# A graph network's four hops: the products and totals on VectorE take their factor from an SBUF column instead of the instruction

## The chip, the core and the metric

The kernel runs on one core of a Trainium2 chip. The metric is the time of one execution on the device in microseconds (us), the median over the runs. The times of single instructions come from one further execution, which the hardware profiler recorded.

## The reference, cut to what matters

Two graph layers follow each other on 50000 nodes with 128 features and 25000 edges (`src`, `dst`). The first layer gives each edge a message, adds the messages up by node, and multiplies with a weight matrix; a layer norm follows. The second layer is the one whose code is changed:

```python
src2 = concat([src, dst]); dst2 = concat([dst, src]); e2 = concat([e, e])      # 50000 directed edges, 4 heads
e2 = e2 / segment_sum(e2, dst2)[dst2]
def f(y): return segment_sum(y[src3] * e3, dst3)      # edges from a node to itself count zero
k1 = f(x); k2 = f(x + k1/3); k3 = f(x + k2 - k1/3); k4 = f(x + k1 - k2 + k3)
y = x + 0.125 * (k1 + 3*(k2 + k3) + k4)
```

Because `f` is linear, the result is a sum of powers of `f`: x + f(x) + f(f(x))/2 + f³(x)/6 + f⁴(x)/24. The kernel computes four such applications in turn and calls each a hop. A last layer norm gives the output.

## The kernel before, in words

A first part (until about 1840 us) sorts the directed edges by the node that they end in, computes the first layer, and builds the tables for the hops. The sorted edges lie as 128 rows of C = 392 columns. Then come four hops (`hop(h)`, h = 0 to 3), and after about 4100 us the last layer norm, in which GpSimd gathers rows once more (L1128).

A hop goes over NB = 49 batches of B = 8 columns, so 128 x 8 edges of 128 features. Each engine has its own list of instructions, written out by hand, and they are tied by semaphores.

- GpSimd (POOL in the profile) issues one indirect DMA per column (L1004), which gathers the 128 rows of the edges' other ends from HBM into one of four buffers `gx`. It may run up to four batches ahead of VectorE (it waits for `z_set`).
- VectorE (DVE) waits for the eight gathers of a batch, then multiplies them by the edge weights `wt` into `zt`. In hop 0 this is four instructions of 128x256 (L1041, one per head, with no wait between them), in hops 1 to 3 one of 128x1024 (L1046). These are called the first product here.
- Then VectorE adds along the row of edges that end in the same node: eight instructions of 128x128 (L1056), the running sums. Each waits for the one before. Their factor is a column of the tile `cont` in SBUF.
- Then one 128x1024 product with `inv` into `us` (L1061), and in hops 1 to 3 the total, `tn = us * share + tp`, again 128x1024 (L1068).
- SyncE (SP) writes `us` and `tn` to HBM and loads `tp`.

All of these are the VectorE instruction `scalar_tensor_tensor`: out = (in0 op factor) op in1. It reads two tensors, both from SBUF here, and a factor. The factor is either a number in the instruction or one value per partition, read from a [128, 1] column in SBUF.

Of the kernel before, what the change touches and what calls it, by code (L numbers as in the profile page):

```python
# [65 lines left out]
def build(nc, x, src, dst, e_in, ea_in, Wf, bf, Wq, Wk, Wa, Wu, bu, out):  # L66
# [9 lines left out]
    with ExitStack() as ctx:  # L76
        def sb(name, shape, dt=F32, stage=None):
            return (stage or ctx).enter_context(nc.sbuf_tensor(name, shape, dt))
# [9 lines left out]
        part = sb("part", [128, Q])  # L88
        after = sb("after", [128, 128])
        ones = sb("ones", [128, ST])  # L90
        first_row = sb("first_row", [128, 128])
        eps_t = sb("eps_t", [128, 1])
        key = sb("key", [128, 2 * NT])
# [15 lines left out]
        wt = sb("wt", [128, C, H])  # L109
        inv = sb("inv", [128, C, H])  # L110
# [64 lines left out]
        with nc.Block() as block:  # L175
# [108 lines left out]
            def _(v):  # L284
# [2 lines left out]
                v.memset(srt[0][:, :], PAD).then_inc(code_set, 1)  # L287
                v.memset(ones[:, :], 1.0).then_inc(const_set, 1)
                v.memset(eps_t[:, :], EPS)
                v.wait_ge(iota_done, 3)  # L290
                v.tensor_copy(pos[:, :], pos_i[:, :]).then_inc(code_set, 1)
                v.tensor_copy(part[:, :], part_i[:, :]).then_inc(code_set, 1)
# [70 lines left out]
                for k in range(1, 17):  # L363
                    v.wait_ge(srt_set, n)
                    t = srt[a]
# [37 lines left out]
                for n in range(NHG):  # L403
                    if n >= 2:
                        v.wait_ge(counted, n - 1)
                    for i in range(HG):
# [3 lines left out]
                        t = v.tensor_scalar(hot_lo[n % 2][:, i, :], pos_h[0:EP, :], part_f[:, 1, c:c + 1], None,  # L410
                                            ALU.is_equal)
# [510 lines left out]
        us = [sb(f"us{i}", [128, B, D], F32, held) for i in range(3)]  # L922
        tp = [sb(f"tp{i}", [128, B, D], F32, held) for i in range(3)]
        tn = [sb(f"tn{i}", [128, B, D], F32, held) for i in range(3)]
# [10 lines left out]
        def hop(h):  # L935
# [4 lines left out]
            share = (1.0, 0.5, 1.0 / 6, 1.0 / 24)[h]  # L940
# [7 lines left out]
            def slot(b, m, n):  # L948

                return n * ((NB - 1 - b % m) // m + 1) + b // m  # L950
# [7 lines left out]
            def by_head(t):  # L958
                return t[:, :, :].rearrange("p j (h f) -> p (j h) f", h=H)

            def per_head(w, cs):
                return w[:, cs, :].rearrange("p j h -> p (j h)").unsqueeze(2).to_broadcast([128, B * H, HF])

            def gxv(i):
                return gx[i][:, 0:B * width].rearrange("p (j f) -> p j f", j=B)

            with nc.Block() as block:
                @block.sync
                def _(sp):
                    for b in range(NB + 1):  # L970
                        if h and b < NB:
                            if b >= 3:
                                sp.wait_ge(tn_set, t0 + b - 2)
                            sp.dma_start(tp[b % 3][:, :, :], rows(so_far, b)).then_inc(t_in[b % 3], 16)
                        if b >= 1:
                            k = b - 1
                            if h < 3:
                                sp.wait_ge(us_set, done + k + 1)
                                sp.dma_start(rows(u[h], k), us[k % 3][:, :, :]).then_inc(u_out[k % 3], 16)
                            if h:  # L980
                                sp.wait_ge(tn_set, t0 + k + 1)
                                sp.dma_start(rows(target, k), tn[k % 3][:, :, :]).then_inc(t_out[k % 3], 16)
                    sp.wait_ge(x_set, x0 + 3)
                    if h < 3:
                        sp.dma_start(u[h][XROW:XROW + 128, :], cross[:, :]).then_inc(x_out, 16)
                        for i in range(3):
                            sp.wait_ge(u_out[i], outs(i, h))
                    else:
                        sp.dma_start(target[XROW:XROW + 128, :], cross[:, :]).then_inc(x_out, 16)
                    if h:  # L990
                        for i in range(3):
                            sp.wait_ge(t_out[i], outs(i, h - 1))
                    sp.wait_ge(x_out, h * 16 + 16)
# [38 lines left out]
                @block.vector  # L1032
                def _(v):
                    for b in range(NB):
                        cs = slice(b * B, (b + 1) * B)
                        z = zt[b % 2]
                        v.wait_ge(g_in[b % 4], (slot(b, 4, h) + 1) * B * 16)
                        if h == 0:
                            for i in range(H):
                                f = slice(i * HF, (i + 1) * HF)  # L1040
                                t = v.scalar_tensor_tensor(z[:, :, f], gxv(b % 4)[:, :, f], 1.0,  # L1041
                                                           wt[:, cs, i].unsqueeze(2).to_broadcast([128, B, HF]),
                                                           ALU.mult, ALU.mult)
                            t.then_inc(z_set, 1)
                        else:
                            v.scalar_tensor_tensor(by_head(z), by_head(gxv(b % 4)), 1.0, per_head(wt, cs),  # L1046
                                                   ALU.mult, ALU.mult).then_inc(z_set, 1)
                        v.wait_ge(z_set, done + b + 1)
                        for j in range(B):
                            c = b * B + j  # L1050
                            if c == 0:
                                continue
                            prev = z[:, j - 1, :] if j else zt[1 - b % 2][:, B - 1, :]
                            if c >= 2:
                                v.wait_ge(run_set, run0 + c - 1)
                            v.scalar_tensor_tensor(z[:, j, :], prev, cont[:, c:c + 1], z[:, j, :], ALU.mult, ALU.add  # L1056
                                                   ).then_inc(run_set, 1)
                        v.wait_ge(run_set, run0 + b * B + B - 1)
                        if h < 3 and b >= 3:
                            v.wait_ge(u_out[b % 3], slot(b, 3, h) * 16)  # L1060
                        v.scalar_tensor_tensor(by_head(us[b % 3]), by_head(z), 1.0, per_head(inv, cs),  # L1061
                                               ALU.mult, ALU.mult).then_inc(us_set, 1)
                        if h:
                            v.wait_ge(t_in[b % 3], slot(b, 3, h - 1) * 16 + 16)
                            if b >= 3:
                                v.wait_ge(t_out[b % 3], slot(b, 3, h - 1) * 16)
                            v.wait_ge(us_set, done + b + 1)
                            v.scalar_tensor_tensor(tn[b % 3][:, :, :], us[b % 3][:, :, :], share, tp[b % 3][:, :, :],  # L1068
                                                   ALU.mult, ALU.add).then_inc(tn_set, 1)

                    v.wait_ge(carried, h + 1)
                    v.tensor_tensor(cross[:, :].rearrange("p (h f) -> p h f", h=H),
                                    bank[0][:, 0:D].rearrange("p (h f) -> p h f", h=H),
                                    inv_first[:, :].unsqueeze(2).to_broadcast([128, H, HF]), ALU.mult
                                    ).then_inc(x_set, 1)
                    v.wait_ge(x_set, x0 + 1)
                    v.scalar_tensor_tensor(cross_sum[:, :], cross[:, :], share, cross_sum[:, :], ALU.mult, ALU.add
                                           ).then_inc(run_set, 1)
                    v.wait_ge(first_in, h * 16 + 16)
                    v.wait_ge(run_set, run0 + C)  # L1080
                    if h < 3:
                        v.tensor_tensor(cross[:, :], cross[:, :], first_u[:, :], ALU.add).then_inc(x_set, 2)
                    else:
                        v.tensor_tensor(cross[:, :], cross_sum[:, :], first_u[:, :], ALU.add).then_inc(x_set, 2)
# [90 lines left out]
```

## Time and profile before

| | |
|---|---|
| median of 3 runs | 4589.34 us (4587.24 to 4590.71) |
| profiled execution, its own time | 4611.0 us |
| its span (first to last instruction) | 4608.9 us |
| VectorE busy | 2438.1 us (53%) |
| GpSimd busy | 3161.3 us (69%) |
| first gather of hop 0, last gather of hop 3 | 1840.2 us, 4080.7 us |

Busy time is the time in which an engine executes an instruction; the short pauses in which GpSimd prepares the next DMA do not count as busy. An engine's idle time matters only where another engine waits for it.

### The profile page before, as it was taken

The page shows a single profiled execution, that of the slowest core. Times are in us where ns is not written, and L with a number is a line of the kernel's source. Part 1 is how long each engine was busy: PE and PEld are TensorE (multiplying, and loading weights), DVE is VectorE, ACT ScalarE, POOL GpSimd, SP SyncE. Part 2 cuts the span into 40 slices and gives each one's busy share as a digit, 9 for nine tenths or more (in the row PEclk, how much of TensorE's full clock was granted, in tenths as well). Part 3 has the DMA queues.
Part 4 walks back from the last instruction along what each step waited for, and adds up shares of the span by engine and source line. Part 5 has one row for each costly group of instructions (what it writes and reads, how often), then busy time and mean ns, then how long its engine had stood idle before and what let it go on. Part 6 is the DMA issues. An engine that isn't in the chain of part 4 may idle for free. (4 is left out here: it accounts for less than half of the span.)

```text
span 4608.9 us, 25791 instructions
## 1 busy us (share of the span) xinstructions
PE 930.8 (20%) x5636; PEld 763.5 (17%) x5636; DVE 2438.1 (53%) x7329; ACT 608.4 (13%) x1752; POOL 3161.3 (69%) x2952
## 2 busy tenths in 40 slices
PE   0364666665667700000000000000000000000000
PEld 0123556555545500000000000000000000000000
DVE  6895444444468902455445555455554555543333
ACT  0001111111147810000000000000000000003333
POOL 0004877877867775777767777677776777767776
PEclk9997877788789955555555555555555555555555
DMA  8002333333357810333335555455554444445555
GB/s 249 13 1 54 64 65 69 65 66 69 60 168 246 256 26 4 95 99 96 99 100 187 188 183 183 157 188 183 183 189 147 138 139 144 140 122 157 157 160 142
DMA packets 294505, 581.90 MB, mean 126 GB/s; under 512 B 118824, under 2 KB 147294, under 8 KB 294349
## 3 DMA queue, kind: packets, MB, share of 16 engines
q1 hardware_dynamic: 172669, 383.36, 24.5%
q0 software_dynamic: 116128, 169.55, 18.4%
q10 hardware_dynamic: 5552, 27.34, 1.8%
q8 instruction: 44, 0.72, 0.1%
q14 instruction: 112, 0.92, 0.1%
HBM read 332.26 MB, written 247.75 MB: 126 GB/s over the span
## 5 line engine op out<-in xcount | busy, mean ns | idle before, releaser
L1004 POOL DMA_INDIRECT gx<-u,far_row x1176 | 1290.0, 1097 | 391.6 <-issue 357.8
L1056 DVE SCALAR_TENSOR_TENSOR zt<-zt,cont 128x128 f32<-128x128 f32 x1564 | 551.2, 352 | 55.5
L1046 DVE SCALAR_TENSOR_TENSOR zt<-gx,wt 128x1024 f32<-128x1024 f32 x147 | 180.5, 1228 | 682.2 <-DMA gx<-u,far_row 682.2
L1004 POOL DMA_INDIRECT gx<-x,far_i x392 | 405.6, 1035 | 147.6 <-issue 119.2
L552 POOL DMA_INDIRECT xs<-in_x_dram,node_idx x196 | 195.9, 999 | 438.2 <-POOLq L175 378.8
L800 POOL DMA_INDIRECT edge_s<-edge_d,edge_id x392 | 376.0, 959 | 141.0 <-issue 132.1
L1021 PE MATMUL bank<-zt,chain 128*128 128x128 f32 x8 | 3.2, 501 | 2267.1 <-DVE zt L1056 2267.1
L1128 POOL DMA_INDIRECT o_ag<-total,fin_idx x390 | 369.9, 948 | 129.9 <-issue 118.6
L1021 PEld LDWEIGHTS bank<-zt,chain 128*128 128x128 f32 x8 | 2.0, 312 | 2268.1 <-DVE zt L1056 2268.1
L544 POOL DMA_INDIRECT agg<-summed,sc_idx x196 | 316.6, 1615 | 81.1 <-issue 58.1
L734 ACT ACTIVATE o_log_v<-o_mv,eps_t 128x6 f32<-128x6 f32 x66 | 19.7, 299 | 2052.8 <-DVE o_mv L727 2052.8
L647 DVE TENSOR_SCALAR neg<-bank 128x512 f32<-128x512 f32 x49 | 33.9, 692 | 485.1 <-PE bank L597 485.1
L1061 DVE SCALAR_TENSOR_TENSOR us<-zt,inv 128x1024 f32<-128x1024 f32 x196 | 240.0, 1224 | 6.8
L556 POOL DMA_INDIRECT xd<-in_x_dram,node_idx x196 | 201.0, 1026 | 59.8 <-issue 59.8
L1148 DVE SCALAR_TENSOR_TENSOR o_res<-o_xc,o_ag 128x768 f32<-128x768 f32 x66 | 62.6, 948 | 317.6 <-issue 285.0
L1041 DVE SCALAR_TENSOR_TENSOR zt<-gx,wt 128x256 f32<-128x256 f32 x196 | 70.3, 420 | 250.0 <-DMA gx<-x,far_i 250.0
L1068 DVE SCALAR_TENSOR_TENSOR tn<-us,tp 128x1024 f32<-128x1024 f32 x147 | 180.2, 1226 | 20.8 <-DVE us L1061 0.5
L574 PE MATMUL bank<-za,same 128*128 128x132 f32 x1568 | 184.6, 276 | 3.0 <-DVE za L680 3.0
L574 PEld LDWEIGHTS bank<-za,same 128*128 128x128 f32 x1568 | 180.2, 190 | 3.2 <-issue 3.2
L753 ACT ACTIVATE normed<-res,shift,rstd 128x128 f32<-128x128 f32 x391 | 156.8, 480 | 0.0
L753 ACT ACTIVATE o_normed<-o_res,o_shift,o_rstd 128x128 f32<-128x128 f32 x391 | 156.4, 478 | 0.0
L410 DVE TENSOR_SCALAR hot_lo<-pos_h,part_f 125x512 f16<-125x512 f16 x400 | 139.3, 348 | 0.0
(182 smaller groups left out, 3140.9 us busy)
## 6 DMA issues: line engine op xcount, KB each, us to landing
u<-us SPq DMA_DIRECT2D x147, 512.0 KB, 2.6
total<-tn SPq DMA_DIRECT2D x147, 512.0 KB, 3.3
tp<-total SPq DMA_DIRECT2D x98, 512.0 KB, 5.2
agg<-zero ACTq DMA_DIRECT2D x49, 544.5 KB
ag<-agg SPq DMA_DIRECT2D x65, 396.0 KB
x<-normed SPq DMA_DIRECT2D x65, 387.0 KB
o_xc<-x SPq DMA_DIRECT2D x65, 387.0 KB, 5.0
tp<-u SPq DMA_DIRECT2D x49, 512.0 KB, 5.9
```

The lines of the kernel that those rows point to most:

```text
L544: g.indirect_dma_start(agg[:, :], bass.IndirectOffsetOnAxis(ap=sc_idx[:, s * Q + j:s * Q + j + 1], axis=0), summed[s % 2][:, j, :], None, ...
L552: g.indirect_dma_start(xs[s % 3][:, j, :], None, x[:, :], bass.IndirectOffsetOnAxis(ap=node_idx[:, s * Q + j:s * Q + j + 1], axis=0)).then ...
L556: g.indirect_dma_start(xd[s % 3][:, j, :], None, x[:, :], bass.IndirectOffsetOnAxis(ap=node_idx[:, c:c + 1], axis=0)).then_inc(x_in[s % 3] ...
L574: t = pe.matmul(r_bank[b // 2][:, b % 2 * AW:(b % 2 + 1) * AW], same[s % 2][:, a, b * 128:(b + 1) * 128], za[s % 2][:, a, :], start=(a == ...
L753: t = act.activation(normed[s % 2][0:P, r, 0:D], res[s % 4][0:P, r, :], ACT.Identity, bias=shift[s % 4][0:P, r:r + 1], scale=rstd[s % 4][0 ...
L800: g.indirect_dma_start(edge_s[:, c, :], None, edge_d[:, :], bass.IndirectOffsetOnAxis(ap=edge_id[:, c:c + 1], axis=0)).then_inc(edge_in, 16)
L1004: g.indirect_dma_start(gx[b % 4][:, j * width:(j + 1) * width], None, source[:, :], bass.IndirectOffsetOnAxis(ap=idx[:, c:c + 1], axis=0)) ...
L1046: v.scalar_tensor_tensor(by_head(z), by_head(gxv(b % 4)), 1.0, per_head(wt, cs), ALU.mult, ALU.mult).then_inc(z_set, 1)
L1056: v.scalar_tensor_tensor(z[:, j, :], prev, cont[:, c:c + 1], z[:, j, :], ALU.mult, ALU.add).then_inc(run_set, 1)
L1061: v.scalar_tensor_tensor(by_head(us[b % 3]), by_head(z), 1.0, per_head(inv, cs), ALU.mult, ALU.mult).then_inc(us_set, 1)
L1068: v.scalar_tensor_tensor(tn[b % 3][:, :, :], us[b % 3][:, :, :], share, tp[b % 3][:, :, :], ALU.mult, ALU.add).then_inc(tn_set, 1)
L1128: g.indirect_dma_start(ag[s % 4][0:P, r, 0:D], None, total[2][:, :], bass.IndirectOffsetOnAxis(ap=at, axis=0)).then_inc(o_row[s % 4], 16)
```

## The change

The number 1.0 in the three products (L1041, L1046, L1061) becomes the first column of `ones`, a tile that the kernel already has. The number `share` in the total (L1068) becomes a column of a new 128x4 tile `shares`, which four small memsets fill at the program's start. What is computed stays the same. No instruction is moved on any engine, none is taken away, and the four memsets are the only ones added. The new tile moves the tiles allocated behind it by 32 bytes.

```diff
+        shares = sb("shares", [128, 4])
...
                 v.memset(eps_t[:, :], EPS)
+                for i in range(4):
+                    v.memset(shares[:, i:i + 1], (1.0, 0.5, 1.0 / 6, 1.0 / 24)[i])
                 v.wait_ge(iota_done, 3)
...
-                                t = v.scalar_tensor_tensor(z[:, :, f], gxv(b % 4)[:, :, f], 1.0,
+                                t = v.scalar_tensor_tensor(z[:, :, f], gxv(b % 4)[:, :, f], ones[:, 0:1],
                                                            wt[:, cs, i].unsqueeze(2).to_broadcast([128, B, HF]),
                                                            ALU.mult, ALU.mult)
...
-                            v.scalar_tensor_tensor(by_head(z), by_head(gxv(b % 4)), 1.0, per_head(wt, cs),
+                            v.scalar_tensor_tensor(by_head(z), by_head(gxv(b % 4)), ones[:, 0:1], per_head(wt, cs),
                                                    ALU.mult, ALU.mult).then_inc(z_set, 1)
...
-                        v.scalar_tensor_tensor(by_head(us[b % 3]), by_head(z), 1.0, per_head(inv, cs),
+                        v.scalar_tensor_tensor(by_head(us[b % 3]), by_head(z), ones[:, 0:1], per_head(inv, cs),
                                                ALU.mult, ALU.mult).then_inc(us_set, 1)
...
-                            v.scalar_tensor_tensor(tn[b % 3][:, :, :], us[b % 3][:, :, :], share, tp[b % 3][:, :, :],
+                            v.scalar_tensor_tensor(tn[b % 3][:, :, :], us[b % 3][:, :, :], shares[:, h:h + 1], tp[b % 3][:, :, :],
                                                    ALU.mult, ALU.add).then_inc(tn_set, 1)
```

## Rows read from the trace of the kernel before

**Rows 1.** Page, part 1: busy us, share of the span, instructions.

```profile
PE 930.8 (20%) x5636; PEld 763.5 (17%) x5636; DVE 2438.1 (53%) x7329; ACT 608.4 (13%) x1752; POOL 3161.3 (69%) x2952
```

**Rows 2.** Waits, 1840 to 4100 us: us in total, times, longest.

```profile
DVE zt L1046 <- DMA gx<-u,far_row: 682.2, 147, 20.6
POOL gx L1004 <- issue: 477.0, 1564, 0.3
```

**Rows 3.** Groups, 1840 to 4100 us: busy us, mean ns | idle before.

```profile
L1004 POOL DMA_INDIRECT gx<-u,far_row x1176 | 1290.0, 1097 | 391.6 <-issue 357.8 <-ACTq L967 33.8
L1056 DVE SCALAR_TENSOR_TENSOR zt<-zt,cont 128x128 f32<-128x128 f32 x1564 | 551.2, 352 | 55.5
L1004 POOL DMA_INDIRECT gx<-x,far_i x392 | 405.6, 1035 | 147.6 <-issue 119.2 <-POOLq L781 28.4
...
L1046 DVE SCALAR_TENSOR_TENSOR zt<-gx,wt 128x1024 f32<-128x1024 f32 x147 | 180.5, 1228 | 682.2 <-DMA gx<-u,far_row 682.2
...
L1041 DVE SCALAR_TENSOR_TENSOR zt<-gx,wt 128x256 f32<-128x256 f32 x196 | 70.3, 420 | 250.0 <-DMA gx<-x,far_i 250.0
...
L1077 DVE SCALAR_TENSOR_TENSOR cross_sum<-cross,cross_sum 128x128 f32<-128x128 f32 x4 | 1.2, 292 | 0.1
```

**Rows 4.** Timeline, one batch of hop 3: start us, us, engine, line.

```profile
3738.52 1.23 DVE L1046 SCALAR_TENSOR_TENSOR zt<-gx,wt 128x1024 f32<-128x1024 f32 x1 [4.35 <-DMA gx<-u,far_row]
3739.05 1.52 POOL L1004 DMA_INDIRECT gx<-u,far_row  x1 [0.30 <-issue]
...
3742.89 1.22 DVE L1061 SCALAR_TENSOR_TENSOR us<-zt,inv 128x1024 f32<-128x1024 f32 x1
3743.38 1.55 POOL L1004 DMA_INDIRECT gx<-u,far_row  x1 [0.30 <-issue]
3744.25 1.23 DVE L1068 SCALAR_TENSOR_TENSOR tn<-us,tp 128x1024 f32<-128x1024 f32 x1
3745.23 1.06 POOL L1004 DMA_INDIRECT gx<-u,far_row  x1 [0.30 <-issue]
...
3749.77 1.23 DVE L1046 SCALAR_TENSOR_TENSOR zt<-gx,wt 128x1024 f32<-128x1024 f32 x1 [4.29 <-DMA gx<-u,far_row]
```

**Rows 5.** Timeline, one batch of hop 0.

```profile
1958.68 1.43 DVE L1041 SCALAR_TENSOR_TENSOR zt<-gx,wt 128x256 f32<-128x256 f32 x4 [5.01 <-DMA gx<-x,far_i]
1959.80 1.13 POOL L1004 DMA_INDIRECT gx<-x,far_i  x1 [0.30 <-issue]
...
1963.25 1.22 DVE L1061 SCALAR_TENSOR_TENSOR us<-zt,inv 128x1024 f32<-128x1024 f32 x1
1963.74 1.55 POOL L1004 DMA_INDIRECT gx<-x,far_i  x1 [0.30 <-issue]
```

**Rows 6.** Timeline before the hops; L859's factor is a column.

```profile
1317.36 0.61 DVE L859 SCALAR_TENSOR_TENSOR xa<-ag,decay,xc 128x128 f32<-128x128 f32 x2
...
1317.73 1.06 POOL L800 DMA_INDIRECT edge_s<-edge_d,edge_id  x1 [0.30 <-issue]
```

**Rows 7.** Timeline, a gather that starts just behind an L1056.

```profile
3340.42 0.41 DVE L1056 SCALAR_TENSOR_TENSOR zt<-zt,cont 128x128 f32<-128x128 f32 x1
3340.51 0.95 POOL L1004 DMA_INDIRECT gx<-u,far_row  x1 [0.31 <-issue]
...
3551.11 0.35 DVE L1056 SCALAR_TENSOR_TENSOR zt<-zt,cont 128x128 f32<-128x128 f32 x1
3551.23 1.05 POOL L1004 DMA_INDIRECT gx<-u,far_row  x1 [0.30 <-issue]
```

**Rows 8.** Timeline, a gather that starts just behind an L1046.

```profile
2648.25 1.22 DVE L1046 SCALAR_TENSOR_TENSOR zt<-gx,wt 128x1024 f32<-128x1024 f32 x1 [6.08 <-DMA gx<-u,far_row]
2648.30 2.00 POOL L1004 DMA_INDIRECT gx<-u,far_row  x1 [0.30 <-issue]
```

**Rows 9.** Timeline, at the program's start.

```profile
5.09 0.06 DVE L289 MEMSET eps_t<- 128x1 f32 x1
```

**Rows 10.** Waits, 9 to 24 us: us in total, times, longest.

```profile
DVE rows_f L322 <- DMA rows_i<-in_dst_dram: 13.6, 1, 13.6
```

## The prediction, made before the changed kernel was run

> **What bounds the kernel now.** I read the page first: GpSimd is busy 69% of the span, more than any other engine [rows 1]. Then the waits of the four hops, 1840 to 4100 us. Before a gather GpSimd waits only for its own issue, 0.30 us each, 477 us over 1564 gathers; apart from the hops' first gathers it waits for no other engine. VectorE in turn waits 682 us for gathers in front of L1046 [rows 2]. So the hops last as long as GpSimd needs for 1568 gathers.
>
> Then the groups: a gather takes 1097 ns on average in hops 1 to 3 and 1035 ns in hop 0 [rows 3], but the undisturbed ones in the timeline take 0.95 us [rows 7]. The timeline shows where the rest comes from. In a batch of hop 3 a gather starts at 3739.05, inside L1046, which ends at 3739.75. It takes 1.52 us and ends at 3740.57, 0.82 behind L1046's end. The one at 3743.38 starts inside L1061 (end 3744.11) and ends at 3744.93, again 0.82 behind. The one at 3745.23 starts inside L1068 (end 3745.48) and ends at 3746.29, 0.81 behind [rows 4]. So a gather that starts while such a VectorE instruction runs stands still until it ends, and then needs its last 0.82 us. A free gather would have reached this point 0.95 - 0.82 = 0.13 us after its start.
>
> Over the batch that is 0.57 + 0.60 + 0.11 = 1.28 us lost, and 8 x (0.95 + 0.30) + 1.28 = 11.28 us, against 3749.77 - 3738.52 = 11.25 measured [rows 4]. Over all, the stops cost 1176 x (1.097 - 0.947) + 392 x (1.035 - 0.947) = 176 + 34 = 211 us, with 0.947 for the 0.95. The running sums have the very form of the changed ones, and 60 is my value.
>
> **Does the column form stop GpSimd too?** Yes: L859 takes its factor from a column. Two of them end at 1317.97; the gather of 1317.73 takes 1.06 us and ends at 1318.79, 0.82 behind [rows 6]. So do the running sums: a gather that starts 0.12 us behind the start of an L1056 (3551.11, end 3551.46) takes 1.05 us and ends 0.82 behind that end [rows 7].
>
> The Trainium skill, SBUF — State Buffer, section "Who interferes with whom", says that an instruction with two SBUF inputs contends with GpSimd's reads only, and infers that issuing a DMA, which needs the write side, isn't stopped by it. By that rule the stops and with them the change would cost nothing; the rows say otherwise, and they decide.
>
> **Hops 1 to 3.** Take the batch of rows 4 with 60 ns more on each of L1046, L1061 and L1068. The gather in L1046 is released 0.06 later. The next gathers and the running sums both hang on that end, so their distance stays, and a gather again starts 0.49 into L1061, whose end is now 0.12 later. Again both sides hang on that end, and L1068 releases GpSimd 0.18 later. Where no gather falls into L1046 the sum is the same, since L1061 and L1068 still stop one and their ends are 0.12 and 0.18 later against the batch's start. 147 batches x 0.18 = 26.5 us.
>
> One thing works against it: which engine is first. In the immediate form a gather that starts 0.05 behind L1046's start is already stopped (2.00 us) [rows 8]; in the column form one at 0.09 goes free and VectorE waits instead (0.41 in place of 0.35), while one at 0.12 is stopped [rows 7]. So the tensors are read about 0.06 later, behind the column. Gathers start every 1.25 us and their place against L1046 varies from batch to batch; if evenly, 0.06 / 1.25 = 5% of 147 batches, 7, now slip in front of L1046 and escape. Each wins about a whole gather, 1.1 us: -8 us. Hops 1 to 3: +18 us.
>
> **Hop 0.** The four L1041 last 1.43 us together: 0.42 the last, and a distance of about 0.34 from start to start (3 x 0.34 + 0.42 = 1.44). A gather starts 1.12 into them, inside the fourth, is released at 1.43 and ends 2.25 behind the batch's start. L1061 starts 3.14 behind the end of the fourth; the gather that it stops starts 3.63 behind that end, so 0.49 into it [rows 5]. With 0.06 more each, the third ends at 2 x 0.40 + 0.48 = 1.28 and the fourth at 1.68. The gather at 1.12 is now in the third, is released at 1.28, and its successor reaches L1061 at 1.28 + 3.63 = 4.91. L1061 begins at 1.68 + 3.14 = 4.82. That is 0.09 inside: exactly where the gather wins the race by rows 7. So two outcomes per batch:
> - Stopped: L1061 ends 4 x 0.06 + 0.06 = 0.30 later and holds GpSimd until then. Batch +0.30; over 49 batches +14.7 us.
> - Escaped: the gather is issued first, the next comes 1.25 later, at 6.16, when L1061 has less than 0.13 left. The batch has no stop but at most 0.1 in the third: 8 x 1.25 + 0.05 = 10.05 us. Before it was 10.0 + 0.18 + 0.60 = 10.78 in rows 5, and by the group's mean 8 x (1.035 + 0.304) = 10.71. So -0.66, over 49 batches -32 us.
>
> Which one depends on where the gather starts. If it comes later than 1.28 - 0.13 = 1.15 it isn't stopped by the third and reaches L1061 at 4.91 to 5.0, up to 0.18 inside, which is stopped. The mean place follows from the group: 34 us over 49 batches is 0.70 a batch, less 0.60 for L1061 is 0.10 at the fourth, so a mean start of 1.43 - 0.13 - 0.10 = 1.20. So somewhat more than half come too late to escape. With a third escaping: 0.67 x 0.30 - 0.33 x 0.66 = -0.02 a batch. Hop 0: 0 us, and I keep +15 and -32 as ends.
>
> **The rest.** The four memsets take 0.06 us each [rows 9] and lie before a wait of VectorE of 13.6 us for `rows_i` [rows 10]: nothing; without this cover 0.24 us. The hops' ends, where VectorE's last batch lies on the path, get 3 x 0.18 + 0.30 = 0.8 us. Tiles that lie 32 bytes further on could change how fast DMAs land; GpSimd waits for no landing within a hop, so it would act only through the places of the gathers against L1046: a few us either way, in the range. Nothing is queued newly behind a wait, and SP's writes leave 0.1 to 0.3 us later, with 11 us between batches.
>
> **Sum.** 18 + 0 + 1 = +19 us: 4611.0 + 19 = 4630 for a profiled execution. That one lies 21.7 above the median of the runs, so 4589.3 + 19 = 4608 us. A measurement of this kernel can tell about 0.2%, 9.2 us, from no change: the bounds are 4580 and 4598.5.
>
> **Rivals.**
> - Hop 0 stays stopped throughout (column cost under 55 ns, or gathers later than I think): 18 + 15 + 1 = +34, up to +42 with no escapes in hops 1 to 3: 4623 to 4631. A cost that grows with the elements lies here too, and above: 480 ns on the 3 x 147 long forms of hops 1 to 3 would be 212 us; I hold it for near nothing. For: a race decided by 10 ns. 0.22.
> - Hop 0 escapes throughout, the one that ends on the other side: at 0.06 or more per L1041, once the gather starts before 1.15 in all batches, GpSimd passes in front of L1061. -32 + 18 + 1 = -13: 4576 us. It is faster from about two thirds of the batches on if the others gain little; against it speaks the mean start of 1.20. 0.09.
> - The gains cancel: part of hop 0 escapes, about half, and more than 7 batches of the other hops: +0 to +9, 4589 to 4598. Also here: the column costs nothing in the long forms. 0.17.
> - The column form doesn't stop GpSimd, as the skill's page would have it for all of them: the 211 us come back but for the running sums, about 4380 us. Rows 6 and 7 speak against it. 0.02.
> - The forecast, 4599 to 4622: 0.50.
>
> **Numbers.** Slower: 0.50 + 0.22 = 0.72. Faster: 0.09 + 0.02 = 0.11. Within 0.2%: 0.17. The range, 4582 to 4631, holds the forecast, the stopped hop 0 and the cancelling, leaves out the full escape, and is that wide because hop 0 has ends of +15 and -32; the forecast's own is 4599 to 4622.
>
> **What would show it.** L1046, L1061 and L1068 at about 1286 ns, L1041 at 480. The gathers' mean in hops 1 to 3: 18 us over 1176 is +15 ns, 1112; up to 1120 without escapes. In hop 0 1035 if a third escapes, 1072 if none, 950 if all; a spread between batches of 10.05 and 11.0 us. Released gathers still end 0.82 behind VectorE's end. After 4100 us nothing changes. Wrong would be: long forms that take 1226 as before, gathers of 0.95 us inside a running L1061, or a hop 0 with one kind of batch only.

## The result and the profile after

The changed kernel takes 4626.35 us (median of 4 runs, 4618.09 to 4634.81), the kernel before 4590.02 us in the same runs (4587.24 to 4596.11). The ratio is 1.0077 with a 95% interval of 1.006 to 1.0094: 28 to 43 us slower, 35 in the middle. The profiled execution took 4634.81 us, its span is 4632.8 us.

The page's groups after the change, each with its busy time in us, the mean of one instruction in ns, and the idle time before them (`...` stands for groups left out):

```profile
L1007 POOL DMA_INDIRECT gx<-u,far_row x1176 | 1298.2, 1104 | 391.3 <-issue 357.6
L1059 DVE SCALAR_TENSOR_TENSOR zt<-zt,cont 128x128 f32<-128x128 f32 x1564 | 551.7, 353 | 55.5
L1049 DVE SCALAR_TENSOR_TENSOR zt<-gx,ones,wt 128x1024 f32<-128x1024 f32 x147 | 189.0, 1285 | 666.7 <-DMA gx<-u,far_row 666.7
L1007 POOL DMA_INDIRECT gx<-x,far_i x392 | 415.1, 1059 | 147.5 <-issue 119.2
...
L1064 DVE SCALAR_TENSOR_TENSOR us<-zt,ones,inv 128x1024 f32<-128x1024 f32 x196 | 252.0, 1286 | 7.0
...
L1044 DVE SCALAR_TENSOR_TENSOR zt<-gx,ones,wt 128x256 f32<-128x256 f32 x196 | 82.2, 480 | 243.6 <-DMA gx<-x,far_i 243.6
L1071 DVE SCALAR_TENSOR_TENSOR tn<-us,shares,tp 128x1024 f32<-128x1024 f32 x147 | 188.7, 1284 | 19.8 <-DVE us L1064 0.5
```

All line numbers are 3 higher than before in the hops. The column costs 60 ns at 256 elements a partition (420 to 480) and 57 at 1024 (1228 to 1285) [rows 3], so it is paid once per instruction and doesn't grow with the length. The running sums, which had a column already, stay at 353. VectorE is busy 39.6 us longer in all (2477.7 us against 2438.1) and still waits 667 us for gathers. The gathers, which set the time, went from 1035 to 1059 ns in hop 0 and from 1097 to 1104 in hops 1 to 3.

A batch of hop 3 in the timeline (start, length):

```profile
3740.87 1.28 DVE L1064 SCALAR_TENSOR_TENSOR us<-zt,ones,inv 128x1024 f32<-128x1024 f32 x1
3741.35 1.62 POOL L1007 DMA_INDIRECT gx<-u,far_row  x1 [0.30 <-issue]
3742.29 1.28 DVE L1071 SCALAR_TENSOR_TENSOR tn<-us,shares,tp 128x1024 f32<-128x1024 f32 x1
3743.28 1.11 POOL L1007 DMA_INDIRECT gx<-u,far_row  x1 [0.30 <-issue]
```

Against [rows 4] the gather starts at the same place in the product, 0.48 us in, takes 1.62 in place of 1.55, and ends at 3742.97, again 0.82 behind the product's end. The one in the total takes 1.11 in place of 1.06.

And hop 0, first a batch of the common kind, then one of the few others:

```profile
2055.16 1.69 DVE L1044 SCALAR_TENSOR_TENSOR zt<-gx,ones,wt 128x256 f32<-128x256 f32 x4 [4.88 <-DMA gx<-x,far_i]
2056.39 0.94 POOL L1007 DMA_INDIRECT gx<-x,far_i  x1 [0.30 <-issue]
...
2060.02 1.28 DVE L1064 SCALAR_TENSOR_TENSOR us<-zt,ones,inv 128x1024 f32<-128x1024 f32 x1
2060.13 1.99 POOL L1007 DMA_INDIRECT gx<-x,far_i  x1 [0.30 <-issue]
...
2066.28 0.48 DVE L1044 SCALAR_TENSOR_TENSOR zt<-gx,ones,wt 128x256 f32<-128x256 f32 x1 [4.97 <-DMA gx<-x,far_i]
```

```profile
1979.35 1.67 DVE L1044 SCALAR_TENSOR_TENSOR zt<-gx,ones,wt 128x256 f32<-128x256 f32 x4 [5.05 <-DMA gx<-x,far_i]
1980.42 1.02 POOL L1007 DMA_INDIRECT gx<-x,far_i  x1 [0.31 <-issue]
...
1984.16 1.34 DVE L1064 SCALAR_TENSOR_TENSOR us<-zt,ones,inv 128x1024 f32<-128x1024 f32 x1
1984.24 0.95 POOL L1007 DMA_INDIRECT gx<-x,far_i  x1 [0.30 <-issue]
...
1989.28 0.88 DVE L1044 SCALAR_TENSOR_TENSOR zt<-gx,ones,wt 128x256 f32<-128x256 f32 x2 [3.78 <-DMA gx<-x,far_i]
```

In the first, the gather of 2056.39 (1.23 us into the four products) isn't stopped at all, and the one that reaches L1064 0.11 behind its start stands for 1.05 us, nearly the whole product: the batch takes 11.12 us, from the start of its first product to that of the next batch. In the second the gather is stopped a little by the third product, reaches L1064 0.08 behind its start, is first, and VectorE waits: 1.34 in place of 1.28; the batch takes 9.93 us. Only 3 of the 49 batches are of this kind, where I had expected a third. In 29 the gather comes 0.10 to 0.13 behind the start of L1064 and stands. In 16 a gather that starts 1.25 to 1.31 into the four products is stopped by the fourth of them, and the gather that reaches L1064 then comes about 0.48 behind its start (once 0.87) and is stopped too. The stopped batches take 10.99 us on average, where the mean before was 10.73.

### The profile page after: what moved, and what is told of

Its sections match the earlier page's. It is cut to its first block and busy times, and to the rows that moved or that the text cites. A ratio compares the mean times of both kernels' runs of the same rounds, so it can differ in the third digit from the quotient of the medians.

```text
span 4632.8 us, 25795 instructions
## 1 busy us (share of the span) xinstructions
PE 943.7 (20%) x5636; PEld 773.4 (17%) x5636; DVE 2477.7 (53%) x7333; ACT 609.0 (13%) x1752; POOL 3175.6 (69%) x2952
## 5 line engine op out<-in xcount | busy, mean ns | idle before, releaser
L1007 POOL DMA_INDIRECT gx<-u,far_row x1176 | 1298.2, 1104 | 391.3 <-issue 357.6
L1049 DVE SCALAR_TENSOR_TENSOR zt<-gx,ones,wt 128x1024 f32<-128x1024 f32 x147 | 189.0, 1285 | 666.7 <-DMA gx<-u,far_row 666.7
L1007 POOL DMA_INDIRECT gx<-x,far_i x392 | 415.1, 1059 | 147.5 <-issue 119.2
L1064 DVE SCALAR_TENSOR_TENSOR us<-zt,ones,inv 128x1024 f32<-128x1024 f32 x196 | 252.0, 1286 | 7.0
L1044 DVE SCALAR_TENSOR_TENSOR zt<-gx,ones,wt 128x256 f32<-128x256 f32 x196 | 82.2, 480 | 243.6 <-DMA gx<-x,far_i 243.6
L1071 DVE SCALAR_TENSOR_TENSOR tn<-us,shares,tp 128x1024 f32<-128x1024 f32 x147 | 188.7, 1284 | 19.8 <-DVE us L1064 0.5
```

Of the source, the lines that this page charges most:

```text
L1007: g.indirect_dma_start(gx[b % 4][:, j * width:(j + 1) * width], None, source[:, :], bass.IndirectOffsetOnAxis(ap=idx[:, c:c + 1], axis=0)) ...
L1049: v.scalar_tensor_tensor(by_head(z), by_head(gxv(b % 4)), ones[:, 0:1], per_head(wt, cs), ALU.mult, ALU.mult).then_inc(z_set, 1)
L1064: v.scalar_tensor_tensor(by_head(us[b % 3]), by_head(z), ones[:, 0:1], per_head(inv, cs), ALU.mult, ALU.mult).then_inc(us_set, 1)
```

## Experiments

In the table and the text below, "gather time" is the gathers' busy time plus their issue pauses in the group's row. For the kernel before it is 405.6 + 119.2 = 524.8 us in hop 0 and 1290.0 + 357.8 = 1647.8 us in hops 1 to 3 [rows 3]; for the changed one 534.3 and 1655.8 us. Each comes from one profile. Profiles of kernels with the same hops 1 to 3 (numbers in the instructions) differ by up to 10 us there (1637.6 to 1647.8), and the first gather starts anywhere from 1831 to 1850 us, whatever the change. So single differences of a few us in one hop say nothing, and the ratio, from several runs each, judges the whole kernel.

| kernel | factor in | hop 0, us | hops 1 to 3, us | ratio to before, 95% |
|---|---|---|---|---|
| before | number | 524.8 | 1647.8 | |
| changed | column | 534.3 | 1655.8 | 1.0077 (1.006 to 1.0094) |
| e1_same_places | column | 537.1 | 1662.5 | 1.0079 (1.0061 to 1.0097) |
| e2_tile_only | number | 522.9 | 1639.2 | 0.9992 (0.9982 to 1.0003) |
| e3_hop0_only | column in hop 0 | 534.1 | 1637.6 | 1.0031 (1.0017 to 1.0044) |
| e4_hops123_only | column in hops 1 to 3 | 523.1 | 1668.7 | 1.0055 (1.0035 to 1.0075) |
| e5_l1041_only | column in L1041 | 536.4 | 1644.0 | 1.0014 (0.9999 to 1.003) |
| e8_nudge | column | 516.5 | 1664.5 | 1.0039 (1.0023 to 1.0055) |
| e9_stores_moved | number | 524.2 | 1644.5 | 0.999 (0.9971 to 1.001) |
| e10_gathers_moved | number | 524.4 | 1647.0 | 0.9991 (0.9971 to 1.001) |
| e6_psum | number | 489.0 | 1518.3 | 0.9657 (0.9619 to 0.9695) |
| e7_psum_column | column | 489.1 | 1525.6 | 0.9674 (0.9639 to 0.9708) |
| e11_no_double_read | number | 489.7 | 1468.7 | 0.9542 (0.9501 to 0.9584) |
| e12_no_double_read_column | column | 489.0 | 1467.1 | 0.9539 (0.9499 to 0.9578) |

**The same change with all tiles in their old places** (e1_same_places). The profile of the changed kernel had a hop 3 that was shorter than before, in these group rows of hop 3 alone, first before, then changed:

```profile
L1004 POOL DMA_INDIRECT gx<-u,far_row x392 | 426.2, 1087 | 130.6 <-issue 119.4 <-ACTq L967 11.2
```

```profile
L1007 POOL DMA_INDIRECT gx<-u,far_row x392 | 417.4, 1065 | 130.5 <-issue 119.3 <-ACTq L970 11.2
```

The new tile moves all tiles behind it by 32 bytes, so I took this shift away:

```diff
-        eps_t = sb("eps_t", [128, 1])
+        eps_t = sb("eps_t", [128, 5])       # the four shares in columns 1 to 4
...
-        shares = sb("shares", [128, 4])
```

> The whole change, but the four factors lie in spare columns of the eps_t tile, so that every tile keeps the address that it had before the change. Theory A (what the column costs acts only through the ends of VectorE's instructions, at which a stopped gather is released): hop 0 about 9 us longer than before, hops 1 to 3 about 6 to 9 us each, in all +27 to +36 us over the kernel before. Theory B (the new tile's 32 bytes act too, through how fast DMAs land): then hop 3, which got 9 us shorter in the changed kernel, gets 6 to 9 us longer here, the gather of hop 3 lands in 4.4 us as before and not in 4.1, and the 7 us that came before the first hop are gone.

4629.81 us, ratio 1.0079. Hop 0 is 12.3 us longer than before, hops 1 to 3 14.7. The cost of the change doesn't come from the shift. Hop 3 fits neither theory: both wanted it 6 to 9 us longer than before, so 432 to 435 us of gathers' busy time, and it is 425.2, as before:

```profile
L1006 POOL DMA_INDIRECT gx<-u,far_row x392 | 425.2, 1085 | 130.5 <-issue 119.3 <-ACTq L969 11.2
```

**The shift alone** (e2_tile_only):

```diff
+        shares = sb("shares", [128, 4])     # and its four memsets; all factors stay numbers
```

> The kernel before with the new tile and its four memsets, which nothing reads: only the addresses of the tiles behind it move by 32 bytes. Theory A: no change, within 3 us in every hop. Theory B: hop 3 about 15 us shorter than before with gathers that land in about 4.1 us, and the first hop starts about 7 us later, so in all about -8 us.

4593.32 against 4595.68 us, ratio 0.9992: no change that can be told. Hop 3 did get 15.3 us shorter, 410.9 us busy against 426.2, as theory B had it, but hops 1 and 2 got longer, so that hops 1 to 3 together are 8.6 us shorter, and the first gather starts at 1838.5 us, not 7 us later than the 1840.2 of before:

```profile
L1007 POOL DMA_INDIRECT gx<-u,far_row x392 | 410.9, 1048 | 130.6 <-issue 119.3 <-ACTq L970 11.2
```

**Hop 0 alone, and the other hops alone** (e3_hop0_only, e4_hops123_only): the kernel of e1_same_places with the number put back in the other hops.

In short form:

```diff
# e3_hop0_only
+ ... ones[:, 0:1] if h == 0 else 1.0, per_head(inv, cs)      # L1061; L1041 with the column
# e4_hops123_only
+ ... ones[:, 0:1] if h else 1.0, per_head(inv, cs)           # L1061; L1046, L1068 with the column
```

> The columns in hop 0 alone (L1041 and L1061), addresses as before. Theory A: hop 0 9 to 15 us longer, most batches at about 11.0 us in place of 10.74, a few at 10.0 where the gather comes first; hops 1 to 3 unchanged; in all +9 to +15 us. Rival (the hop 0 part was a shift of what lies before it): hop 0 unchanged.

> The columns in hops 1 to 3 alone, addresses as before. Theory A: hop 0 unchanged, 0.18 us for each of 147 batches, so up to 26 us, less what gathers win that now come in front of the first product: +18 to +26 us. Theory B says the same here, with 6 to 9 us in each hop, hop 3 among them. If hop 3 gets shorter here too, it is not the addresses but the place of the gathers against the longer product.

e3: ratio 1.0031, 8 to 20 us; its hop 0 is 534.1 us, 9.3 above before, and its hops 1 to 3, with the numbers of before, are 10.2 us shorter, which no cause here explains. e4: ratio 1.0055, 16 to 35 us; its hop 0 is 523.1 us (524.8 before), and hops 1 to 3 are 20.9 us longer. The two parts add up to the whole (1.0086 against 1.0077 and 1.0079). In e4 hop 3 is as long as before (426.2 us busy), so the hop 3 of the changed kernel wasn't the rule for columns either.

**The race at L1061, from two sides** (e5_l1041_only, e8_nudge). The column stays in the four L1041 alone:

```diff
-   ... gxv(b % 4)[:, :, f], 1.0,
+   ... gxv(b % 4)[:, :, f], ones[:, 0:1],       # L1041 only, nothing else changed
```

> The column in hop 0's four L1041 alone; L1061 has its number back, so it reads its tensors from about 0.05 us behind its start and not from about 0.10. Theory A: the gather reaches L1061 about 0.11 us behind its start, as in the changed kernel, and is stopped in every batch; the batch gets 4 x 0.06 = 0.24 us longer, 10.98 in place of 10.74, hop 0 +12 us. Rival (only the ends of L1061 matter, not what lies before it): hop 0 unchanged.

Hop 0: 536.4 us, +11.6, as expected; the whole kernel 1.0014 (0.9999 to 1.003), where the 12 us would be 1.0025, inside the interval. In 43 batches a gather comes 0.07 to 0.12 behind the start of L1061, and all 43 are stopped, since this L1061 has its number; in 5 more it comes later and is stopped as well:

```profile
2038.71 1.22 DVE L1061 SCALAR_TENSOR_TENSOR us<-zt,inv 128x1024 f32<-128x1024 f32 x1
2038.80 1.95 POOL L1004 DMA_INDIRECT gx<-x,far_i  x1 [0.30 <-issue]
```

For the other side, I added an instruction to the kernel of e1_same_places, to bring L1061 a little behind the gather:

```diff
+                        if h == 0:
+                            v.memset(spare_col[:, :], 0.0)      # [128, 1], read by nothing
                         v.scalar_tensor_tensor(by_head(us[b % 3]), by_head(z), ones[:, 0:1], per_head(inv, cs),
```

> The kernel e1_same_places with one more instruction, a memset of one column that nothing reads, just ahead of L1061 in hop 0. It makes L1061 start 0.03 to 0.06 us later. Theory A: a gather that came 0.11 us behind L1061's start now comes 0.05 to 0.08 behind it, is first, and runs free in 0.95 us; of 49 batches about 30 go at 10.0 us in place of 11.0, so hop 0 gets about 25 to 30 us shorter than in e1_same_places, although VectorE has more to do. Rival (no race; a gather is stopped wherever it falls into L1061): hop 0 as in e1_same_places or 3 us longer.

Hop 0: 516.5 us against 537.1 in e1_same_places, 20.6 us less, with more work on VectorE. 22 of 49 batches now escape, not 30. In the trace's own nanoseconds the latest gather that runs free comes 89 ns behind the product's start, the earliest that is stopped 92 ns:

```profile
1901.12 1.28 DVE L1066 SCALAR_TENSOR_TENSOR us<-zt,ones,inv 128x1024 f32<-128x1024 f32 x1
1901.14 0.06 DVE L1065 MEMSET spare_col<- 128x1 f32 x1
1901.21 2.01 POOL L1007 DMA_INDIRECT gx<-x,far_i  x1 [0.30 <-issue]
...
2061.38 1.34 DVE L1066 SCALAR_TENSOR_TENSOR us<-zt,ones,inv 128x1024 f32<-128x1024 f32 x1
...
2061.47 0.94 POOL L1007 DMA_INDIRECT gx<-x,far_i  x1 [0.30 <-issue]
...
2081.40 1.33 DVE L1066 SCALAR_TENSOR_TENSOR us<-zt,ones,inv 128x1024 f32<-128x1024 f32 x1
...
2081.47 0.95 POOL L1007 DMA_INDIRECT gx<-x,far_i  x1 [0.30 <-issue]
```

The memset is recorded beside the product, not ahead of it, so it moved the product only a little: the middle one of the gathers now comes 92 ns behind its start, against 118 in e1_same_places. The whole kernel agrees with the hop: ratio 1.0039, where e1_same_places has 1.0079. In the rows, a gather 0.07 behind the start of this column form is free and VectorE is held (1.33 for 1.28). The other two pairs both stand 0.09 apart in these rounded rows, and they are the edge itself: in this hop 3 ns (89 against 92) decide between 0.94 and 2.01 us. At 0.09 behind the number form, in e5, the gather is stopped for a whole microsecond.

**One tensor from PSUM** (e6_psum, e7_psum_column). If it is the second tensor read from SBUF that stops a gather, it must be enough to read one of the two from elsewhere. PSUM is the core's other memory, which VectorE can read and write. In short form (e7_psum_column has the columns besides):

```diff
+        rt = [psum[:, i * 1024:(i + 1) * 1024]... for i in range(2)]     # running sums
+        wt_p = psum[:, 2176:2176 + C * H]...                              # copy of wt, made once
-    z = gx * 1.0 * wt ;  z[j] = z[j-1] * cont + z[j] ;  us = z * 1.0 * inv
+    z = gx * 1.0 * wt_p ; r[j] = r[j-1] * cont + z[j] ; us = r * 1.0 * inv
```

> The kernel before, with the numbers in the instructions, but the edge weights wt are read from a copy in PSUM and the running sums are written to PSUM, so that the first product, the running sums and the product with inv each read one tensor from SBUF; only the total (L1068) still reads two. Theory A (a gather is stopped by an instruction that reads two tensors from SBUF): the gathers stay at 0.95 us beside all but the total, each batch loses at most the total's 0.1 to 1.1 us; hops 1 to 3 at 10.0 to 11.0 us a batch, hop 0 at 10.0; about 120 to 200 us faster than before. Rival (any long VectorE instruction stops a gather, whatever it reads): no gain, about as before.

> The kernel e6_psum with the columns of the change. Theory A: a column costs time only where an instruction stops a gather. Hop 0 stays at 10.0 us a batch, so the change costs nothing there; in hops 1 to 3 only the total is left to stop one, and its end moves 0.18 us, so within plus 26 and minus 26 us of e6_psum, depending on which gather the total meets. Rival (the column's 60 ns cost time by making VectorE late): +40 us over e6_psum.

e6 takes 4446.12 us, ratio 0.9657. Its gathers:

```profile
L1009 POOL DMA_INDIRECT gx<-u,far_row x1176 | 1160.6, 987 | 391.5 <-issue 357.7 <-ACTq L972 33.8
L1009 POOL DMA_INDIRECT gx<-x,far_i x392 | 369.9, 944 | 147.5 <-issue 119.1 <-POOLq L782 28.3
```

In hop 0, 944 ns is the free gather: no stop is left, although the products take the time that they took before (L1041's form 416 ns, L1061's 1225). They still write to SBUF, so it is the second tensor read there that stops a gather, not the length and not the write. In hops 1 to 3 only the total stops gathers, 116 of them. e7, with the columns, takes 4453.33 us, 7.2 more, which the overlapping intervals of the two ratios don't tell from nothing; in the profiles hops 1 to 3 are 7.3 us longer (1525.6 against 1518.3), where the total is left to stop gathers; its hop 0 is the same to 0.1 us, where the change costs 9 to 12 us otherwise.

```profile
L1011 POOL DMA_INDIRECT gx<-u,far_row x1176 | 1167.9, 993 | 391.6 <-issue 357.7 <-ACTq L974 33.9
L1011 POOL DMA_INDIRECT gx<-x,far_i x392 | 369.9, 944 | 147.5 <-issue 119.2 <-POOLq L784 28.4
```

**Stores or gather buffers: what moved hop 3?** (e9_stores_moved, e10_gathers_moved).

```diff
# e9_stores_moved
+        pad = sb("pad", [128, 8], F32, held)       # ahead of us, tp, tn
# e10_gathers_moved
+        pad0 = sb("pad0", [128, 8], F32, held)     # ahead of gx and zt
+        pad = sb("pad", [128, 56], F32, held)      # ahead of us, tp, tn: 256 bytes in all
```

> The kernel before with 32 unused bytes ahead of us, tp and tn, so that these tiles alone move by 32 bytes and start at multiples of 256. In e2_tile_only, where all tiles behind the new one had moved, hop 3 took 530 us; with addresses as before it took 538 to 546 in three profiles. Theory B1 (the stores and loads of these tiles go faster, and with them the gathers land earlier): hop 3 at 530 us, landing at 4.1 us. Rival (noise of the landings, or the gather buffers): hop 3 at 538 to 546 us. Hops 0 to 2 within 5 us of before for both.

> The counterpart: the gather buffers gx and the sums zt move by 32 bytes, and us, tp and tn by 256, so that they keep their place within 256 bytes. Theory B1: hop 3 at 538 to 546 us as before. Theory B2 (the gathers' own landings depend on the buffers' place): hop 3 at 530 us. If both this one and e9_stores_moved are at 538 to 546, the 530 us of e2_tile_only were chance.

Neither changes the time (0.999 and 0.9991). Hop 3 takes 537.7 us in e9 and 545.6 in e10, with the pauses (530.3 in e2_tile_only); its gathers are busy 418.4 and 426.2 us:

```profile
L1005 POOL DMA_INDIRECT gx<-u,far_row x392 | 418.4, 1067 | 130.6 <-issue 119.3 <-ACTq L968 11.3
```

```profile
L1006 POOL DMA_INDIRECT gx<-u,far_row x392 | 426.2, 1087 | 130.5 <-issue 119.3 <-ACTq L969 11.2
```

Neither brings back the 410.9 us of e2_tile_only, so B1 and B2 aren't shown. Whether the two short hops 3 (e2 and the changed kernel) are chance or need both shifts at once stays open; it is 9 to 15 us in one hop of one profile, and about 8 us of the whole kernel at most by e2's interval.

The traces do show where in hop 3 the difference lies. A stopped gather ends about 0.82 us behind the end of the instruction that stopped it, so each can be put down to one. The stops at the first product lose 21.3 us before, 6.9 in e2 and 7.8 in the changed kernel, and 14 to 23 in the other seven kernels that read two tensors from SBUF. The stops at the product with `inv` and the total together are alike in all kernels with numbers there, 32.7 to 34.5 us. In the two short ones the gathers also land earliest (median from issue to landing from 3540 to 4080 us: 2.8 and 2.9 us, 3.0 to 3.1 in the other eight). Earlier landings let the first product start earlier, so that less of it lies behind the gather's start; that this is the reason, and why they land earlier, is not shown.

**No double read at all** (e11_no_double_read, e12_no_double_read_column).

In short form:

```diff
-    us = r * 1.0 * inv ;   tn = us * share + tp
+    usp = r * 1.0 * inv ;  tn = usp * share + tp ;  ScalarE: us = copy(usp)     # usp in PSUM
```

> e6_psum with the last instruction of that kind taken away: the product with inv is written to PSUM, the total reads it there and tp in SBUF, and ScalarE copies it to us in SBUF for the store. No instruction of the hops reads two tensors from SBUF, numbers in the instructions. Theory A: every gather at 0.95 us, 10.0 us a batch in all four hops, about 490 us each; 50 us less than e6_psum, about 4395 us. Rival (the total's stops in e6_psum stand for a bound that comes next, such as the stores): hops 1 to 3 stay at 505 us.

> The change made to e11_no_double_read: all products and totals take the factor from a column. Theory A: without a stop the 60 ns of each instruction lie wholly beside the gathers, so 0 us, within 3 us of e11_no_double_read in every hop. Rival (the column itself costs time on the path): +0.18 us for 147 batches and +0.30 for 49, +41 us.

e11 takes 4400.97 us, e12 4398.44 us. The gathers of e12, and the instructions whose factor is a column:

```profile
L1013 POOL DMA_INDIRECT gx<-u,far_row x1176 | 1109.6, 944 | 391.1 <-issue 357.5 <-POOLq L976 22.5 <-ACTq L976 11.1
L1013 POOL DMA_INDIRECT gx<-x,far_i x392 | 369.8, 943 | 147.5 <-issue 119.2 <-POOLq L784 28.4
L1086 DVE SCALAR_TENSOR_TENSOR psum<-psum,ones,inv 128x1024 f32<-128x1024 f32 x196 | 253.3, 1292 | 6.9
L1093 DVE SCALAR_TENSOR_TENSOR tn<-psum,eps_t,tp 128x1024 f32<-128x1024 f32 x147 | 188.7, 1283 | 19.6 <-DVE psum L1086 0.5
```

The columns still cost their 60 ns in each instruction (the product with `inv` takes 1232 ns in e11), and the time is the same: the cost is there, and none of it is on the path. With no double read the kernel is 4.6% faster than before, with numbers or with columns.

## Why the prediction was right, and where it was off

- **What bounds the hops.** GpSimd's gathers, and the stops in them. Shown: with the stops away all four hops take 8 x (0.944 + 0.304) = 9.98 us a batch.
- **The cost of one instruction**, 60 ns and independent of its length. Measured 57 to 62 by the groups' means.
- **The column form stops gathers too, until its end, and 0.82 us are left then.** It does so in the rows above, unless the gather comes first. The rule of the Trainium skill that I had set beside it (SBUF — State Buffer, section "Who interferes with whom") holds in its first part: a second tensor from SBUF is what collides with GpSimd, and one tensor from PSUM ends it (e6, e11). I had drawn from the page that the stops and with them the change would cost nothing; the gathers' stops cost 214 us here (gather time before against e11). But these gathers also read their row numbers from SBUF (`far_i`, `far_row`), and the first part of the rule covers a GpSimd instruction that reads SBUF. So the runs don't refute the page's inference about the write side: no run separates the reading of the row numbers from the rest of the issue.
- **Hops 1 to 3, +18 us.** The mean gather time over the six profiles with numbers (before, e2, e3, e5, e9, e10) is 1643.4 us, over the four with columns (changed, e1, e4, e8) 1662.9: +19.5. The single profile of the changed kernel shows +8. The sum was right, one of its two terms wasn't. With each stopped gather put down to its instruction, the stops at the product with `inv` cost 9.8 us more (84.3 to 94.1) and those at the total 7.4 (16.9 to 24.3), 17.2 where the forecast had 2 x 8.8 = 17.6. The stops at the first product cost only 2.9 us more (72.8 to 75.7), where it had 8.8 less 8 for seven batches that escape. But the gathers that start in the first 0.1 us of the first product and go free rise only from 6 to 8 of 147, and the stopped ones rise too, from 120 to 126. What kept that term small is mostly that the gathers start later in the longer product, which the prediction didn't have; single profiles spread from 67 to 80 us there. That the total came out right is in that part luck.
- **Hop 0, 0 us: the step that failed.** It is +11.3 us (523.9 mean of before, e2, e4, e9, e10; 535.2 of changed, e1, e3). The two outcomes and their prices were right: 10.99 us on average for a stopped batch (forecast 11.0), 9.93 to 9.96 for one that escapes (forecast 10.05). The share was wrong: 3 of 49 in the changed kernel, 3 in e3 and none in e1, and not a third. The step that failed is the gather's mean start in the four products, which I took from before (1.20; the trace of before has 1.18) and left in place. After the change it is 1.23. Before, 11 of 48 gathers start ahead of the 1.15 below which a batch can escape, which is already less than a third; after it, 2 do. With 1.23 the third product doesn't stop the gather and the next one reaches the product with `inv` 0.12 behind its start, too late. The three that escape come at 0.084 to 0.089, a few ns ahead of the edge. The rival "hop 0 stays stopped" had +15 us and was the case, but for those three. Its neighbour, the rival "hop 0 escapes throughout", had an error of its own: two thirds of the batches escaping would give 14.7 - 0.67 x 47 + 19 = +2 us, the old time and not a faster one.
- **The sum**, 4608 us with 4582 to 4631, against 4626. As a difference it is +19 against +35: 16 us low, 11 of them by hop 0 and 1.5 by hops 1 to 3; the rest lies inside the measured 28 to 43. The forecast's own range, 4599 to 4622, missed; the wide one holds 4626 because it took in the stopped hop 0.
- **Memsets and places of tiles:** nothing that can be told in the time (e2), as said.

## What to carry to other kernels

Where GpSimd issues indirect DMAs all the time, as here, look at the VectorE instructions that read two tensors from SBUF beside them: from the moment at which one stops a DMA, its end is on the path, even on an engine that is half idle. Read one of the two from PSUM before saving on the instructions themselves: here that was worth about 200 us, and a change that cost 35 us then cost nothing that can be told. A factor that is the same in all partitions is cheaper as a number in the instruction, by about 60 ns each here.

## What the runs showed of the hardware

- A product of 1024 elements with a column starts to hold GpSimd off about 0.09 us behind its recorded start: the earliest gather that is stopped comes at 92 ns (e8_nudge), the latest that is free at 89 there and at 94 in the changed kernel. With a number the two are 46 ns (before) and 44 (e3_hop0_only), for a running sum, with its column, 100 (e1_same_places) and 98 (e3_hop0_only). A gather ahead of that point isn't slowed, and VectorE takes up to 0.07 us longer; one that is stopped just behind it stands for 1.06 us, in a running sum for 0.12.
- The column itself doesn't count as a second tensor: with a column and one tensor from SBUF, the other from PSUM, no gather is stopped (944 ns in hop 0 of e7_psum_column, 943 and 944 in e12).
- So an added instruction can make a kernel faster (e8_nudge, hop 0 by 20.6 us), and the same 60 ns on each of five instructions cost a batch of hop 0 nothing (e12 against e11), 0.26 us where it stays stopped, or win it about 0.8 where it escapes (9.93 to 9.96 against 10.73).
- The product with `inv` takes 1232 ns with a PSUM input and a PSUM output (e11) against 1224 with SBUF alone, and a running sum 359 against 352: the way around costs VectorE almost nothing.
